# Cross-attention, one core: values and sums once per pair of head groups, small scalars moved to ScalarE, and the first and last transfers in a new order

## The reference

```python
Q = split_heads(query @ Wq + bq)          # query: x (16, 512, 512)
K = split_heads(key @ Wk + bk)            # key = value: ctx_1024 (16, 77, 512)
V = split_heads(value @ Wv + bv)          # 16 heads of 32
scores = jnp.einsum('bhqd,bhkd->bhqk', Q, K) / np.sqrt(D_K)
attn = jax.nn.softmax(scores, axis=-1)
ctx = jnp.einsum('bhqk,bhkd->bhqd', attn, V)
out = ctx @ Wo + bo
return _layer_norm(out + query, ln_gamma, ln_beta)
```

## Time and profile before

| | |
|---|---|
| device time, three runs | 612.38, 612.84, 614.36 us (median 612.84) |
| the profiled execution | 612.02 us, of it 610.2 us from first to last instruction (the span) |
| PE busy | 593.9 us, 97% |
| DVE, POOL, ACT busy | 82%, 73%, 60% |
| granted TensorE clock, mean | 0.995 of full |

### The profile page before, as it was taken

One profiled execution on the slowest core, in us unless ns is written; L12 is line 12 of the kernel. 1 busy time (PEld: TensorE's weight loads), 2 busy tenths in 40 slices (PEclk: granted clock), 3 DMA queues, 4 the chain that ended last, 5 costly groups with the idle time before them and its releaser, 6 DMA issues.

```text
span 610.2 us, 12052 instructions
## 1 busy us (share of the span) xinstructions
PE 593.9 (97%) x3342; PEld 430.0 (70%) x3342; DVE 498.6 (82%) x914; ACT 364.3 (60%) x674; POOL 444.0 (73%) x395
## 2 busy tenths in 40 slices
PE   9999999999999999999999999999999999999892
PEld 6877677777777777777777777777777777777562
DVE  5535588888898888898888888888888888889775
ACT  5622355566666667666666666666666666655562
POOL 1363045468888888888888888888888888878785
PEclk9999999999999999999999999999999999999998
DMA  8959799979898998989797979798798979896523
GB/s 287 337 217 234 188 246 251 220 167 221 193 233 214 215 218 205 225 221 221 211 219 201 219 208 224 210 220 226 193 221 219 222 206 225 198 226 163 170 78 124
DMA packets 93392, 129.58 MB, mean 212 GB/s; under 512 B 49936, under 2 KB 49936, under 8 KB 93360
## 3 DMA queue, kind: packets, MB, share of 16 engines
q1 hardware_dynamic: 74016, 93.80, 60.7%
q10 hardware_dynamic: 19344, 35.40, 22.2%
HBM read 53.94 MB, written 24.35 MB: 128 GB/s over the span
## 4 chain that ended last, share of the span: by engine, by line
PE 93%; SPq 2%; DMA 2%; DVE 1%; issue 1%; ACT 0%; DVEq 0%
PE p_q L628 28%; PE p_o L696 27%; PE p_s L660 11%; PE p_v L671 10%; PE p_a L646 6%; PE pk L314 5%; PE p_o L113 3%; SPq L565 1%; DMA z<-nmt 1%; PE pk L322 1%; SPq L560 1%; PE p_a L713 1%; DMA k_low<-ktl 1%; PE p_den L679 1%; PE p_q L713 0%
## 5 line engine op out<-in xcount | busy, mean ns | idle before, releaser
L769 ACT ACTIVATE prob<-p_s 77x512 f32<-77x512 f32 x256 | 144.0, 592 | 102.0 <-PE p_s L660 92.2
L1120 POOL TENSOR_TENSOR cl<-cxt,ch 128x512 fp32r<-128x512 f32 x64 | 83.2, 1300 | 108.4 <-ACT ch L794 108.4
L984 DVE TENSOR_REDUCE nm<-p_a 128x4 f32<-128x308 f32 x256 | 117.2, 476 | 51.8 <-PE p_a L646 50.5
L939 DVE TRANSPOSE_TENSOR_REDUCE part<-prob 96x64 f32<-96x2048 f32 x64 | 146.4, 2287 | 1.6 <-issue 1.3
L784 ACT ACTIVATE qh<-p_q,bq_col 128x512 fp32r<-128x512 f32 x64 | 44.0, 687 | 111.5 <-PE p_q L628 111.5
L628 PE MATMUL p_q<-xl,wqh 128*128 128x512 f32 x256 | 101.2, 395 | 0.0
L628 PE MATMUL p_q<-xh,wql 128*128 128x512 f32 x256 | 101.0, 395 | 0.0
L628 PE MATMUL p_q<-xh,wqh 128*128 128x512 f32 x256 | 101.0, 394 | 0.0
L660 PE MATMUL p_s<-z,ks 97*77 97x512 f32 x256 | 94.8, 411 | 2.5 <-DMA z<-nmt 2.5
L696 PE MATMUL p_o<-woh,ch 128*128 128x512 f32 x240 | 95.4, 397 | 0.2 <-POOL cl L1120 0.2
L696 PE MATMUL p_o<-wol,ch 128*128 128x512 f32 x240 | 94.7, 394 | 0.0
(11 more groups left out here) (129 smaller groups left out, 933.8 us busy)
## 6 DMA issues: line engine op xcount, KB each, us to landing
z<-qh SPq DMA_DIRECT2D x256, 128.0 KB, 3.5
z<-ql SPq DMA_DIRECT2D x124, 128.0 KB, 4.7
xn<-in_x ACTq DMA_DIRECT2D x60, 256.0 KB, 3.3
out_dram<-y SPq DMA_DIRECT2D x60, 256.0 KB, 4.1
xt<-in_x_t ACTq DMA_DIRECT2D x58, 256.0 KB, 4.8
ks<-k_high SPq DMA_DIRECT2D x32, 154.0 KB, 5.0
cx<-in_ctx_t SPq DMA_DIRECT2D x4, 616.0 KB, 5.8
k_high<-kth SPq DMA_DIRECT2D x4, 616.0 KB, 3.6
```

Of the source, the lines that this page charges most:

```text
L769: nc.scalar.activation(prob[0:S2, j, :], p_s[j % 2][0:S2, :], ACT.Exp, scale=SCALE).then_inc(prob_ready, 1)
L939: nc.vector.tensor_reduce(part[:], prob[0:KP, :, :].rearrange("p h (i r) -> p (h i) r", r=DK), AX_X, ALU.add, apply_transpose=True).then_i ...
L984: nc.vector.tensor_reduce(nm[:, t, g.k % 2:HALF:2], p_a[t % 2][:, 0:HC * S2].rearrange("p (h k) -> p h k", k=S2), AX_X, ALU.max, negate=Tr ...
L1120: nc.gpsimd.tensor_tensor(cl[:, i, g.k % NCH, :], cx[:], ch[:, i, g.k % NCH, :].bitcast(F32), ALU.subtract).then_inc(cl_ready, 1)
```

## The change

**Pairs.** `values` and `sums` are issued only in odd slots, for two chunks at once: `values_of_pair`. `prob`, `part`, `rec` and `cxt` get two halves and `p_v` two banks (the second takes the bank of `p_den`). One `sums` covers both chunks: 32 columns per matmul instead of 16, written to unused columns of bank `p_a[0]`, so the first `rowmax_scores` of an odd slot waits until DVE has inverted them. The last four chunks stay single. DVE sums the even chunk's `prob` between the second and third row maxima of the even slot, inverts a pair at once, and divides one chunk in the odd slot and the other at the front of the next even one; ACT and POOL make `ch` and `cl` in other places accordingly.

**Scalars.** Until slot 63 `ve` and `nmr` are made by ACT (three instructions on 128x1), not by DVE (two).

**Memory.** `wvh` and `wvl` are freed when `attend` begins; `xn`, `gamma_row`, `beta_row`, `bo_row` lie there, so they may be loaded only when the last V tile is summed: at the front of slot 8 in ACT's queue. Wo is loaded into the halves of `cxt`, into `rden` and into `vb`, each of which must be read before its first use.

**Transfers.** The first key block `kb0` is loaded in halves, the first behind the third K store. For the first pair the copies of `ql` are issued by ACT, and SP issues the maxima right behind `qh`. The last stores are in the order of `y_last_done`, with `x_last[0]` at the end.

```diff
-WO_SLOTS = (4, 6)
-ROWS_SLOT = 5
+WO_SLOTS = (4, 5)
+ROWS_SLOT = 8
...
+                if c == 2:
+                    sp.wait_ge(keep["kb0_zeroed"], 1)
+                    for i in range(2):
+                        sp.wait_ge(k_stored[i], 32)
...
+        wo_raw = [cx[:, 0, :], rden[:], vb[:, 1, :], cx[:, 1, :]]
...
-                if g.k % 2 == 0 and g.back(2).valid(NG) and not is_last(g.back(1)):
+                if g.k % 2 == 0 and g.back(2).valid(NG) and not at_edge(g.back(1)):
                     load_maxima(g.back(2))
...
-            sp.wait_ge(y_done, NS - 1)
-            sp.dma_start(out_dram[NS], x_last[0]).then_inc(stored[0], 16)
             for n, t in enumerate((1, 2, 3)):
                 sp.wait_ge(y_last_done, n + 3)
                 sp.dma_start(out_dram[NS + t], x_last[t]).then_inc(stored[t], 16)
+            sp.wait_ge(y_done, NS - 1)
+            sp.dma_start(out_dram[NS], x_last[0]).then_inc(stored[0], 16)
...
+                if t == 0 and g.k % 2 == 1 and g.back(LAG_PV).valid(NG):
+                    pe.wait_ge(rec_ready, g.back(LAG_PV).over(1, 1))
...
+            def values_of_pair(g):
+
+                at_least(pe, cx_ready, g.over(1, -1))
+                values(g.back(1))
+                values(g)
+                pe.wait_ge(part_ready, g.over(1, 1))
+                at_least(pe, rec_ready, g.over(1, -1))
+                at_least(pe, max_ready, g.over(1, LAG_PV, QT) - 1)
+                for j in range(HC):
+                    last = nc.tensor.matmul(den_pair[DK * j:DK * (j + 1), :].rearrange("p (i r) -> p i r", r=QB), sel[:],
+                                            part[:, :, QB * j:QB * (j + 1)], start=True, stop=True)
+                last.then_inc(pv_summed, 2)
...
-                if v.valid(NG) and g.valid(NG):
-                    values(v)
-                    sums(v)
+                if v.valid(NG) and g.valid(NG) and g.k % 2 == 1:
+                    values_of_pair(v)
...
                 if not g.valid(NG):
+                    pe.wait_ge(cx_ready, v.over(1))
                     values(v)
...
+                if g.k % 2 == 0 and w.valid(NG) and not single(w):
+                    ctx_high(w)
                 if s.valid(NG):
                     exp(s, 0)
                     exp(s, 1)
                 if m.valid(NS):
                     square(m)
+                    if g.valid(NG):
+                        variance(m)
...
             def divide(g):
                 i = g.k % 2
+                if g.back(1).is_first():
+                    dve.wait_ge(wo_low, KC)
                 dve.wait_ge(rden_ready, g.over(1, 1))
...
+                if m.valid(NS) and g.valid(NG) and g.k % 2 == 0:
+                    add_residual(m)
+                if g.k % 2 == 0 and w.valid(NG) and not single(w):
+                    spread(w)
+                    divide(w)
...
+                w, e = v.back(1), v.back(2)
+                if g.k % 2 == 0 and e.valid(NG) and not single(e):
+                    ctx_low(e)
+                if g.k % 2 == 0 and w.valid(NG) and not single(w):
+                    ctx_low(w)
                 if g.back(LAG_SCALE).valid(NS):
                     scale(g.back(LAG_SCALE))
```

More of the change, by code:

```diff
@@ L438, in attend @@
                       (p_s[0], prob_ready, NG * HC)]
-        gamma_tail, beta_tail = p_s[1], p_den
+        gamma_tail, beta_tail = p_s[1], p_v[1]
         x_last = [xt[:, 0, :], xt[:, 1, :], bv_row[:], vb[:, B % 2, :]]
@@ L678, in sums @@
                 for j in range(HC):
-                    last = nc.tensor.matmul(p_den[DK * j:DK * (j + 1), 0:QB], sel[:], part[:, QB * j:QB * (j + 1)],
+                    last = nc.tensor.matmul(den_single[DK * j:DK * (j + 1), :], sel[:], part[:, g.k % 2, QB * j:QB * (j + 1)],
                                             start=True, stop=True)
@@ L766, in exp @@
                         act.wait_ge(const_pool, 2)
[L767 to L769 removed]
+                    at_least(act, pv_summed, pair_end(g.back(2)))
+                    at_least(act, part_ready, g.over(1, -1))
+                nc.scalar.activation(prob[0:S2, g.k % 2, j, :], p_s[j % 2][0:S2, :], ACT.Exp, scale=SCALE).then_inc(prob_ready, 1)
             def split_x_high(n):
@@ L852, in slot @@
                     square(m)
-                if g.back(LAG_NORM - 2).valid(NS):
+                    if g.valid(NG):
+                        variance(m)
+                if g.back(LAG_NORM - 2).valid(NS) and not g.back(ROWS_SLOT - 1).is_first() and not g.back(ROWS_SLOT).is_first():
                     load_residual(g.back(LAG_NORM - 2))
@@ L857, in slot @@
                     exp(s, 3)
-                if v.valid(NG):
+                if g.k % 2 == 1 and w.valid(NG) and not single(w):
+                    ctx_high(w)
+                if v.valid(NG) and single(v):
                     ctx_high(v)
+                if g.back(LAG_NORMALIZE).valid(NS) and g.valid(NG):
+                    mean_over_std(g.back(LAG_NORMALIZE))
                 if g.back(LAG_NORMALIZE).valid(NS):
@@ L863, in slot @@
                     split_x_high(Slot(0, KC))
-                if is_last(g):
-                    i = g.k // 2 % 2
-                    act.wait_ge(ql_ready, NG)
-                    for j in range(HC):
-                        act.dma_start(z[DK * 2:DK * 3, i, j, :, :].bitcast(F32),
-                                      ql[DK * j:DK * (j + 1), i, :, :].bitcast(F32)).then_inc(z_in[i], 16)
+                if at_edge(g) and not g.back(1).is_first():
+                    copy_low(g)
                 if n.valid(NG):
@@ L882, in slot @@
                     store_v(i)
-                if g.back(ROWS_SLOT).is_first():
-                    for row, src in ((gamma, "ln_gamma"), (beta, "ln_beta"), (bo, "bo")):
-                        act.dma_start(row[:], a[src].partition_broadcast(P)).then_inc(rows_in, 16)
             run(act, slot, NG + LAG_PV - 1)
@@ L1016, in slot @@
                     q_low(g)
-                if v.valid(NG):
+                if v.valid(NG) and single(v):
                     invert_sums(v)
+                    spread(v)
                     divide(v)
-                if m.valid(NS):
+                if v.valid(NG) and not single(v) and g.k % 2 == 1:
+                    invert_sums(v)
+                    spread(w)
+                    divide(w)
+                if m.valid(NS) and not g.valid(NG):
                     variance_of_squares(m)
```

167 lines of the change are left out of this document (111 added, 56 removed).

## The result

The changed kernel took **609.78 us** (median of five executions, 609.58 to 610.19) against 612.79 for the kernel before on the same chip: ratio 0.9945, 95% interval 0.9927 to 0.9962. It is faster by 3.0 us, 0.5%. The forecast was 606, a gain of 6.8; the 609.8 measured lies at the slow end of its range (601 to 610). The profiled execution took 609.58 us, 607.8 of it span.

A forecast was written before the change was run, and what follows sets the result against it. PE, busy for 97% of the span, was taken to bound the kernel. Span: 610.2 - 8.4 - 2.0 + 2.7 + 2.3 - 0.8 = 604.0; 1.8 more for the execution gives 605.8, predicted as 606 us, range 601 to 610.

The forecast's parts named there:

- The start, -2.0: Start: PE's waits for the first key block (0.5 of 0.63 us) and first maxima (1.36) vanish, saving 2.0 us.
- The drain, +2.3: Slots 64 and 65: `y` comes late behind ACT's issues and POOL's chain, costing 2.3 us, or 0.9 without ACT's delay.
- The scalars, 0: Steady slots: three 128x1 instructions added to ACT, at most 2.1 us per slot, and their removal from DVE are hidden.
- the slack of `rec` and `part` in odd slots: Odd slots: DVE delivers `part` and `rec` 0.7 and 0.6 us before PE needs them, so no wait.
- Pairs: Steady slots: values for two chunks cost PE 2.12 us instead of 2.40, saving 0.28 per pair, 8.4 over 30 pairs.
- does a steady slot still hold: Steady slots: even ones last 7.08 us, odd ones 9.2, without waits; smallest slack 0.1, at the even slot's third score.
- The last stores: End: with the new store order the last store is issued at 606.2 instead of 607.02, saving 0.8 us.
- Wo's buffers: a new wait: Slot 6: the division of chunk 1 waits for POOL's `xl` and two `wol`, delaying PE's `p_o`; costs 2.7 us.
- rival 5: Falling clock: at 2.7 us of idle PE the granted clock might drop, costing a few us, 608; chance 0.17 with Rival 2.
- The row loads at slot 8's front ... 0: Slot 8: five load issues on ACT, about 2.7 us from 101.9, finish just when `qh` is due; costs 0.
- Rival 1: Neither new wait (Wo's split, POOL's lag in the drain) costs: 601 us, about 603.5 with one left; chance 0.24.
- Rival 2: A small wait of 0.1 to 0.2 us per pair takes back 3 to 6: 609 to 612; chance 0.17 with rival 5.

The follow-up runs named there:

- experiment 7: Changed kernel with the first pair's `ql` copies back on SP ahead of the maxima, key block still in halves: median 612.02 us.
- experiment 1: Changed kernel with Wo's chunks 2 and 3 loaded two slots earlier from ACT's queue, split between slot 5's exponentials, `wol` ahead of `xl`: median 611.65 us.
- Experiment 10: experiment 9's kernel plus experiment 6's edit, two of the last pair's four `z<-ql` on SP, `load_last(3)` moved into slot 64: median 602.05 us.
- experiment 6: Changed kernel with chunk 59 spread, divided and made `ch` at the end of slot 63 instead of in slot 64: median 610.04 us.
- experiment 11: Changed kernel with `ve` and `nmr` of all tiles made by DVE again (two instructions per tile, not three on ACT): median 609.59 us.
- Experiment 8: Changed kernel with a pair's sums as two sets of 16-column matmuls instead of one of 32, values still in pairs: median 612.29 us.
- experiment 4: Changed kernel with the old order of the last stores, `x_last[0]` first: median 611.19 us.
- Experiment 5: Changed kernel with Wo's chunks 2 and 3 loaded 2.5 us earlier on SP, split behind slot 5's third and fourth exponentials, `wol` ahead of `xl`: median 605.87 us.
- Experiment 2: Changed kernel with only two of slot 8's five row loads ahead of `qh`, the rest later, and `bo` on its own semaphore: median 607.98 us.
- the last experiment: The changed kernel itself run again, unedited: median 609.81 us, ratio 0.9932 to the kernel before.
- experiment 9: Changed kernel with the edits of Experiment 5 (Wo earlier) and Experiment 2 (row loads spread out) together: median 604.59 us.
- experiment 3: Changed kernel with POOL's add of `bo` ahead of the last pair's `cl` in slot 64: median 609.69 us.

## Why the prediction was off

Right in kind and nearly in size:
- **The start, -2.0.** Measured -2.23, of which 0.5 lies ahead of the first Q matmul, where the profiles of this kernel differ by as much among themselves (39.28 to 39.89). So 1.7 is the change's own, and the nearness to 2.0 is partly luck. Slot 0 is 0.4 shorter (7.00 to 6.58), which fits the key block's halves, but no run undid them; the transfers of the first pair gave 1.2 when undone (experiment 7). `p_s` began at 62.05, forecast 62.2. The Trainium skill, "DMA: Bandwidth & Descriptors", Issuing engines are not separate DMA queues, holds that a second engine saves no more than the time of the issues. The trace agrees, but with four issues on the path that is 1.2 us here and not next to nothing, as the prediction read the rule; experiment 1 is its other side, since transfers issued from ACT delayed SP's.
- **The drain, +2.3.** Measured +2.69, slot 65 longer by 2.4, with `y` behind `xn` as described. `ch` of chunk 59 was done at local 4.9 (forecast 5.1), `xn` at 10.15 (10.2). The prediction put 1.4 of its 2.3 down to ACT's issues. Experiment 10, which halves ACT's `ql` issues, moves the load and divides earlier, gives back 1.0 of the 36.0 with a fall in it; experiment 6, the early division alone, gives back nothing. Neither takes the issues away by itself.
- **The scalars, 0** (experiment 11), and the slack of `rec` and `part` in odd slots: from slot 10 to slot 62 the timeline has no wait of PE there.

Wrong in size:
- **"Pairs", -8.4, measured -7.76**, by two errors that nearly cancel, so that its nearness is luck. A pair's PE work is 2.07, not 2.12, which alone gives 9.8. And "does a steady slot still hold": E was to last 7.08 always; 2.0 us are lost in even slots. The prediction had a slack of 0.1 there as the smallest and set the loss at nothing. In slot 32 `qh` starts 0.59 behind the last Q matmul, in slot 34 0.43 behind, and `p_a` behind `qh` comes 0.12 late (its weight load 0.26), and the third score 0.27. Experiment 11 excludes the three new instructions. Nor is it of the change's making: in the kernel before, `qh` has the same 0.60 in slots 16, 24, 32, 40 and 48 and 0.43 in most others. These five are the first slots in the five passes of the kernel's `Fori` loop; the slots from 56 on, which are written out behind it, have 0.43. Before, `values` and `sums` (1.2 us) stood between the Q matmuls and this `p_a` and hid most of it, and in the changed even slots nothing does. What delays ACT at the head of a pass stays open.
- **Where the 0.33 comes from.** The sum gave it to the two losses of 0.09 and 0.06 and to 0.13 for the sums; measured are 0.09, 0.06, 0.14 for the sums and 0.04 because the sixteen `p_v` take 1.74 and not 1.78. Experiment 8: with two full sets of sums in a row the pair still gains 0.28. So what is paid once is mostly the turn from one form of matmul to the next, for the sums too: their first set takes 0.16, a second one behind it 0.07 (two take 0.23). The Trainium skill, "TensorEngine Tiling (Array Packing)", Key Properties, says that a change of mode drains the engine; the 0.09 lost at the turn from 128*128 to 77*32 agrees, while a drain itself is in no row.
- **"The last stores", -0.8, measured -1.35** (as in experiment 4). The issue of the last store accounts for the 0.8 or 0.9; that the span then ends 0.45 sooner behind it was not in the sum.

The two steps that failed:
- **"Wo's buffers: a new wait", +2.7, measured +4.49.** The wait itself was right: 2.69, slot 6 is 10.0 where the clock stays up, 2.9 over its 7.08. The fall of the clock had been put aside as rival 5, because 1.36 us of idle before showed none. It is part of the term: six of nine profiles with this wait have it, and it costs 1.4 to 1.6 us, or 2.7. POOL's chain, `xl` and two `wol`, ran without a gap from 83.49 to 87.30, as summed (87.45). But the transfer, which the sum left out, was as late: the last chunk's load, issued at 78.53, was there at 85.35, and its `woh` was done 0.07 before POOL came to it. So it was luck that leaving it out did no harm, and a faster POOL alone would have gained nothing. Experiment 5, which moves both, takes the wait away.
- **"The row loads at slot 8's front ... 0", measured 1.76.** I took about 0.54 per issue, though the rows had 0.77, and let them begin with the slot (101.9 in the sum); an issue is 0.78 here and they begin 0.35 into it, so `qh` is 1.4 late. And `beta_row`, which the first add of `bo` waits for by a shared semaphore, was not looked at. Experiment 2 gives back all of it.

By these two the forecast of -6.2 in span loses 3.6; the other terms change it by 0.2. That holds between two profiles, of which the one before has no fall; the medians differ by 3.0 in the result and by 4.0 in the last experiment (609.81 and 613.80). Rival 1 (neither wait costs) was false of the changed kernel; with Wo's wait taken away by experiment 9 and the drain's left, the time is 604.6, where the rival had 603.5 for one wait left. Rival 2's mechanism was there, at 2.0 us instead of 3 to 6. What I call shown is what an edit took away and gave back: Wo's wait, the row loads, the stores, the first pair's transfers, and, in part only, ACT's issues in slot 64. That the clock falls because PE idles was not tested by itself; each fall in these profiles begins near the end of a wait of PE, from 0.8 us before it to 1.9 behind it.

## What to carry to other kernels

A change that saves work in every slot and adds single waits at the start and the end must be costed at both; here three places (slot 6, slots 8 and 9, the drain) took 8.9 us, more than the 7.8 that the pairs gave, and only the shorter start and end (3.6) left a gain. Moving loads, two copies and one division brought 1.2% more, some 7.4 us (ratios 0.9932 and 0.9811 to the same kernel before). A wait of PE can be dearer than its length, since the clock may fall with it: behind the wait in slot 6 that was 0 in three profiles, 1.4 to 1.6 us in five and 2.7 in one, 1.1 on average. Count a queue's issues by their measured price, 0.6 to 0.8 us each here as a rule, and ask for each what compute instruction stands behind it on the same engine.

## What the runs showed of the hardware

- The clock's stretches at half in front of PE's end are all 3.4 or 6.8 us long, and each of the twelve kernels run here has one or two in its profile. There are 18 in the thirteen profiles. 17 go with single waits of 1.7 to 2.8 us, and six of these begin while PE still waits (at 80.33 in experiment 1, where the wait ends at 81.07); the one in experiment 10 stands behind three short waits within 6 us (0.55, 0.43, 0.56). Waits of 1.60 us (experiment 3, slot 8) and 1.36 us (the kernel before) had none behind them. The same wait in the same kernel is followed by one in some executions and not in others (slot 64: none in the changed kernel's first profile, one in the last experiment). The Trainium skill, "TensorE: Matmul & The Clock Gate", Terms, puts the penalty at the time spent at the lower clock times the share of pulses left out, by which 3.4 us cost an estimated 1.7. Slot 6 agrees (1.4 to 1.6); in the drain a fall of 3.4 us cost nothing in four profiles (36.0 to 36.1 us, as without one) and 0.7 in a fifth, since PE would have waited there anyway, and one of 6.8 us cost 1.4 to 1.6.
- With two loads of 256 KB more on ACT's queue, issued while SP's transfers for the next pair were under way, a load that SP issued 4 to 5 us later was there 2.7 us later than without them (experiment 1).
- The issue of one copy of 128 KB held ACT's queue for 0.54 to 0.86 us as a rule, but single ones took 1.16, 1.30, 1.60 and 2.33 (experiments 9, 5, 10, 6). Why is not shown.
- `qh` starts 0.59 to 0.61 us behind the start of the last Q matmul in the first slot of each pass of the loop, 0.51 in the fifth, and 0.43 in all other even slots from 10 to 60, in the kernel before and in every profile behind it.
